# Attention scores of four pairs of heads in one issue, into four PSUM banks, instead of two pairs at a time into two

## The reference

```python
# 1: layer norm, attention with 16 heads of 16 over a sliding window of 128, output projection, MLP (GELU, 1024 wide)
scores = einsum('bhcqd,bhckd->bhcqk', qc, kcat) * scale     # own and previous chunk of 128 keys
out = einsum('bhcqk,bhckd->bhcqd', softmax(where(valid, scores, -inf)), vcat)
# 2: RWKV channel mix:  sigmoid(xr @ W_r.T) * (square(relu(xk @ W_k.T)) @ W_v.T)
# 3: Mamba: in-projection, convolution, then per channel (512) and state (16) over 256 channels of model width
hs = associative_scan((dA, BX)); y = einsum('blen,bln->ble', hs, Cm) + D * xc; out = (y * silu(z)) @ out_proj_w.T
# 4: one expert of 8 for each sequence, chosen by the mean of x: relu(x @ W1[top1] + b1) @ W2[top1] + b2
```

## Time and profile before

| | us |
|---|---|
| median of 3 runs (lowest, highest) | 3230.02 (3225.7, 3231.91) |
| time of the profiled execution | 3228.74 |
| its span, from the first to the last instruction | 3226.9 |
| PE busy / POOL / DVE / ACT | 2898.2 / 2642.7 / 2482.5 / 2391.9 |
| mean granted TensorE clock, as a share of full speed | 0.947 |

### The profile page before, as it was taken

How to read it: one execution, slowest core, us unless ns; L and a number is a source line. 1 busy time by engine, 2 the same in 40 slices (tenths; PEclk the granted TensorE clock), 3 DMA queues, 4 the chain that set the end, 5 groups by cost and what they waited for, 6 DMA issues and landing times.

```text
span 3226.9 us, 54604 instructions
## 1 busy us (share of the span) xinstructions
PE 2898.2 (90%) x17328; PEld 1833.4 (57%) x17328; DVE 2482.5 (77%) x5644; ACT 2391.9 (74%) x5299; POOL 2642.7 (82%) x1590
## 2 busy tenths in 40 slices
PE   5898888899999999999999999999999999988567
PEld 3565455475665656566565656656565655654246
DVE  3256978788787878879787887878787887879980
ACT  4587868787786878778687878878687787855432
POOL 1117999998998989999899989989998998988870
PEclk9999999899999999999999999999999999989788
DMA  3004453446445454644545364444545454455531
GB/s 82 14 35 144 145 164 111 158 146 206 131 143 173 153 182 140 205 145 147 184 127 198 127 210 141 169 153 149 190 128 197 149 179 140 151 182 180 176 124 41
DMA packets 285967, 477.31 MB, mean 148 GB/s; under 512 B 38451, under 2 KB 93363, under 8 KB 285683
## 3 DMA queue, kind: packets, MB, share of 16 engines
q1 hardware_dynamic: 285682, 473.83, 44.7%
HBM read 388.79 MB, written 84.93 MB: 147 GB/s over the span
## 4 chain that ended last, share of the span: by engine, by line
PE 70%; POOL 9%; ACT 8%; issue 6%; DVE 5%; DMA 2%; SPq 1%; ACTq 0%; DVEq 0%; POOLq 0%
PE bank L518 21%; PE bank L526 9%; PE bank L641 7%; PE bank L777 6%; PE bank L763 6%; PE bank L563 6%; PE bank L551 6%; PE bank L716 5%; POOL h_rows L1539 4%; POOL h_rows L1549 4%; PE bank L579 3%; ACT prob L832 2%; PE bank L512 2%; ACT zb L797 2%; DVE h_rows L1315 1%
## 5 line engine op out<-in xcount | busy, mean ns | idle before, releaser
L1539 POOL TENSOR_TENSOR h_rows<-u_rows,b_rows 128x1024 f32<-128x1024 f32 x512 | 1203.3, 2365 | 35.1 <-DMA b_rows<-bc_dram 34.4
L1549 POOL TENSOR_TENSOR h_rows<-h_rows,c_rows 128x1024 f32<-128x1024 f32 x480 | 1129.6, 2365 | 63.7 <-DVE state L1322 49.1
L1003 ACT ACTIVATE bank<-d_rows,a_rep 128x512 f32<-128x512 f32 x1024 | 682.5, 688 | 154.4 <-DMA d_rows<-delta_dram 44.3
L1315 DVE TENSOR_TENSOR_SCAN h_rows<-bank,state,h_rows 128x512 f32<-128x512 f32 x480 | 594.5, 1267 | 44.9 <-ACT bank L1003 30.1
L1315 DVE TENSOR_TENSOR_SCAN h_rows<-bank,h_rows 128x512 f32<-128x512 f32 x480 | 575.0, 1213 | 51.2 <-ACT bank L1003 40.0
L832 ACT ACTIVATE prob<-prob,neg_max 128x256 f32<-128x256 f32 x1024 | 509.4, 504 | 85.9 <-DVE neg_max L1098 85.8
L1098 DVE CUSTOM_DVE_ANT_0 prob<-bank,bands 128x256 f32<-128x256 f32 x896 | 335.9, 417 | 166.3 <-PE bank L551 162.4
L563 PE MATMUL bank<-ident,prob 128*128 128x128 f32 x2048 | 316.1, 281 | 61.3 <-ACT prob L832 55.1
L563 PEld LDWEIGHTS bank<-ident,prob 128*128 128x128 f32 x2048 | 235.8, 142 | 218.9 <-issue 199.7
L716 PE MATMUL bank<-h_rows,sum_n 128*32 128x512 f32 x2048 | 281.6, 625 | 70.7 <-POOL h_rows L1549 58.2
L518 PE MATMUL bank<-nb,w 128*128 128x512 f32 x512 | 270.7, 685 | 15.8 <-ACT nb L790 12.0
(11 more groups left out here) (164 smaller groups left out, 4847.8 us busy)
## 6 DMA issues: line engine op xcount, KB each, us to landing
u_rows<-u_dram SPq DMA_DIRECT2D x256, 256.0 KB, 3.9
d_rows<-delta_dram SPq DMA_DIRECT2D x256, 256.0 KB, 4.1
b_rows<-bc_dram SPq DMA_DIRECT2D x256, 256.0 KB, 3.1
c_rows<-bc_dram SPq DMA_DIRECT2D x256, 256.0 KB, 3.1
w<-in_W SPq DMA_DIRECT2D x28, 1024.0 KB, 7.1
zs_dram<-region_b SPq DMA_DIRECT2D x64, 256.0 KB, 2.8
xc_dram<-region_b SPq DMA_DIRECT2D x64, 256.0 KB, 3.5
u_dram<-region_b SPq DMA_DIRECT2D x64, 256.0 KB, 2.1
```

Of the source, the lines that this page charges most:

```text
L1003: e.activation(banks[at.bank][:, :], d_rows[:, c, :], ACT.Exp, scale=a_rep[:, k:k + 1]).then_inc(filled[at.bank], 1)
L1315: e.tensor_tensor_scan(rows, banks[at.bank][:, :], rows, start, ALU.mult, ALU.add).then_inc(drained[at.bank], 1)
L1539: e.tensor_tensor(half_of(i, b, half), u_rows[:, 2 * half:2 * half + 2, :], twice(b_rows[:, b % 2, :]), ALU.mult).then_inc(bx_ready.sem, 1)
L1549: e.tensor_tensor(rows, rows, twice(c_rows[:, b % 2, :]), ALU.mult).then_inc(hc_ready.sem, 1)
```

## The change

Four pairs are issued together at every eighth beat: the first head of each of the four, then the second head of each. So four row groups follow each other in PE's list, and four banks must be free before the first. The step in which DVE masks each pair stays where it was, so the two later pairs of such a quad hold their banks four beats longer. The functions that decide which scan quads VectorE finishes are rewritten as well (`vector_quads` for `vector_out`), with the same quads as before: none but the odd ones of the last two groups.

```diff
@@ uses_of, attention
         for n in range(32):
             v, odd = divmod(n, 2)
             at = ATT0 + 4 * v
-            out += [(f"s{n}", at, at + 1 + odd), (f"p{n}", at + 5 + odd, at + 6 + 2 * odd)]
+            out += [(f"s{n}", ATT0 + 8 * (n // 4), at + 1 + odd), (f"p{n}", at + 5 + odd, at + 6 + 2 * odd)]
@@ pe_attention
-            def scores_of(v):
-
-                if v == 0:
+            def scores_of(w):
+
+                if w == 0:
                     for name in ("q0", "q1", "k0", "k1"):
                         e.wait_ge(*gone(use(name)))
-                for n in (2 * v, 2 * v + 1):
+                for n in range(QUAD * w, QUAD * w + QUAD):
                     e.wait_ge(*free(use(f"s{n}")))
                 for par in range(2):
-                    for n in (2 * v, 2 * v + 1):
+                    for n in range(QUAD * w, QUAD * w + QUAD):
...
             for beat in range(AFTER - ATT0):
-                if beat % 4 == 0 and beat < 64:
-                    scores_of(beat // 4)
+                if beat % 8 == 0 and beat < 64:
+                    scores_of(beat // 8)
@@ the scan's choice of quads, in words the same as before
-def vector_out(i, b, batches):
-
-    return i >= 2 * batches - 2 and b % 2 == 1
+MIDDLE_QUADS, LAST_QUADS = (), tuple(range(1, QUADS, 2))
+def vector_quads(i, batches):
+
+    return LAST_QUADS if i >= 2 * batches - 2 else MIDDLE_QUADS
```

More of the change, by code:

```diff
@@ L110, with uses_of @@
 )
-def vector_out(i, b, batches):
-    return i >= 2 * batches - 2 and b % 2 == 1
-def uses_of(stage, shared=False):
+MIDDLE_QUADS, LAST_QUADS = (), tuple(range(1, QUADS, 2))
+def vector_quads(i, batches):
+    return LAST_QUADS if i >= 2 * batches - 2 else MIDDLE_QUADS
+def uses_of(stage, quads=()):
     if stage == "attention":
@@ L140, in uses_of @@
     if stage == "scan":
-        return ([(f"d{k}", SCAN0 + 2 * k + DECAY_AT, SCAN0 + 2 * k + (1 if shared and k // 4 % 2 else 0))
+        return ([(f"d{k}", SCAN0 + 2 * k + DECAY_AT, SCAN0 + 2 * k + (1 if k // 4 in quads else 0))
                  for k in range(TILES)]
@@ L179, in schedule @@
     for stage in PLACES:
[L180 to L183, removed]
+        for quads in ({(), MIDDLE_QUADS, LAST_QUADS} if stage == "scan" else {()}):
+            for name, first, last in uses_of(stage, quads):
+                begins.setdefault((stage, quads, first), []).append(name)
+                ends.setdefault((stage, quads, last), []).append(name)
     def earlier(thread, i):
@@ L196, in schedule @@
             _, _, stage, i, step = chain[0]
-            shared = stage == "scan" and vector_out(i, 1, batches)
-            names = begins.get((stage, shared, step), ())
+            quads = vector_quads(i, batches) if stage == "scan" else ()
+            names = begins.get((stage, quads, step), ())
             if len(names) <= len(idle) and not any(c in chains for c in earlier(*key)):
@@ L208, in schedule @@
             signalled[bank] += not (stage == "scan" and name[0] == "y")
-        for name in ends.get((stage, shared, step), ()):
+        for name in ends.get((stage, quads, step), ()):
             idle.append(uses[stage, i, name].bank)
@@ L455, in states_kept, with by_vector @@
             return state_ready.sem, CREDIT + (i // 2) * 2 * QUADS + (2 * QUADS if i % 2 else 2 * b + half + 1)
-        def out_formed(i, b):
[L459 to L463, removed]
+        quads_by = {"vector": [], "gpsimd": []}
+        for i in range(2 * BATCH):
+            for b in range(QUADS):
+                quads_by["vector" if b in vector_quads(i, BATCH) else "gpsimd"].append((i, b))
+        def by_vector(i, b):
+            return b in vector_quads(i, BATCH)
+        def out_formed(i, b):
+            if by_vector(i, b):
+                return hc_by_vector.sem, CREDIT + quads_by["vector"].index((i, b)) + 1
+            return hc_ready.sem, CREDIT + 2 * quads_by["gpsimd"].index((i, b)) + 2
         def fetched_again(i):
@@ L1310, in run_h @@
                 start = state[:, k:k + 1] if i % 2 else 0.0
-                if vector_out(i, k // 4, BATCH):
+                if by_vector(i, k // 4):
                     e.tensor_tensor_scan(banks[at.bank][:, :], banks[at.bank][:, :], rows, start,
@@ L1319, in keep_states @@
                 k = 4 * b + 2 * half
-                if not vector_out(i, b, BATCH):
+                if not by_vector(i, b):
                     e.wait_ge(*gone(use(f"d{k + 1}")))
@@ L1324, in times_c @@
             def times_c(k):
-                at, b, n = use(f"d{k}"), k // 4, k // 8 * 4 + k % 4
-                e.wait_ge(*h_in_bank.at(i - 2 * BATCH + 2, n + 1))
+                at, b = use(f"d{k}"), k // 4
+                e.wait_ge(h_in_bank.sem, CREDIT + 4 * quads_by["vector"].index((i, b)) + k % 4 + 1)
                 if k % 4 == 0:
@@ L1353, in dve_scan @@
                 k = tile_at(step, 1)
-                if k is not None and vector_out(i, k // 4, BATCH):
+                if k is not None and by_vector(i, k // 4):
                     times_c(k)
@@ L1553, in pool_scan @@
                     b = quad_at(step, OUT_AT + 2 * half)
-                    if b is not None and not vector_out(i, b, BATCH):
+                    if b is not None and not by_vector(i, b):
                         times_c(b, half)
```

## The result

The changed kernel takes 3311.82 us (median of 4 runs, 3309.13 to 3312.92) against 3228.86 us for the kernel before on the same chip: a ratio of 1.0255 (95% interval 1.0238 to 1.0271), so 83 us slower. The forecast was 3188 us, the upper end of the range 3248.

The account below looks back on a forecast made before the run. PE was taken to bound the kernel, with scores holding 181.5 us of the chain. A ceiling of 82 us less 23 and 13 for banks and 5 for the first 473 us left 41: 3188 us, range 3135 to 3248.

Parts of the forecast that it names:

- Four row groups side by side: PE's score matmuls: 16 instructions on four row groups take 1.09 us, against 1.06 for a burst of 8.
- The ceiling of 82 us: Most that PE's scores can gain: 45.3% of the 181.5 us they hold on the chain.
- p15: PE step whose bank comes free only after DVE masks pair 16 and runs two scans; 1.8 us in 13 groups.
- d32: A decay on ACT that now waits for a scan, about 1.3 us later than before; costed at nothing.
- The steps that changed places cost nothing: Steps moved in the list were costed at nothing; two ReLUs done earlier release a bank earlier.
- Some five more places, 1 us for the five together: Third and last quads, p27, a w_v product, an in-projection, an expert product get late banks; 13 us for 13 groups.
- 23 + 13 us for the banks: PE's waits for banks over 13 groups: 23 us at p15, 13 us at some five more places.
- the first 473 us: Opening stretch where DVE and ACT set the beat; half of its 10.3 us gain taken off, 5 us in the sum.
- The slower one: Rival: late banks work through a loop of quad, mask, decay, scan, transposes; 32 us slower, 3261 us, chance 0.16.
- The rule of the Trainium skill: Tiling speeds up TensorE but not PSUM evacuation; by it no gain, 3229 us; judged not to apply yet.
- DVE's wait for scores: Sign: DVE's waiting for PE's scores falls to about half of 118.8 us.
- The new wait before L572: Sign: PE waits for DVE's scan (L1324) before this line, near 1.8 us and once for a group.

Follow-up runs that it names:

- e9: The kernel before, with each score matmul taking only the first 128 of its 256 keys; 3162.72 us, ratio 0.979.
- e17: The whole change, with back taking its two banks just ahead of the copies and the expert's first product just ahead of its ReLU; 3268.04 us.
- e2: The change's order of steps, but two bursts, each pair's bank held as in the kernel before, banks handed out anew; 3269.09 us.
- e16: Step list of quads 0, 1, 2, 5, 6 together, but quad 1 in two bursts, its banks held as before, banks handed out anew; 3256.81 us.
- e18: Quads 0, 1, 2, 5, 6 together, others as before, with back taking its two banks later, just ahead of the copies; 3232.55 us.
- e5: The kernel before with only quads 0, 2, 5, 6 issued together, the others in two bursts, banks held as before; 3233.40 us.
- e7: The kernel before with the scan's decays in five SBUF buffers instead of banks, W_r standing in for four other weights; 4089.3 us, ratio 1.2652.

## Why the prediction was wrong

**Four row groups side by side: right.** 1.08 us for 16 instructions, and the line's busy time is 151.2 us where some 150 were expected.

**The ceiling of 82 us: right.** The rate of e9 gives 77. The share of a line in the chain was a good price for removing its time in the one case where no bank was touched.

**p15: right in place and size.** 1.64 us for 1.8, by the named loop, in e17 too. The three parts given for PE's way to p15 sum to 2.50 us, not 2.43, which makes it 1.74. d32, costed at nothing, cost nothing that shows: PE's wait behind the exponentials fell from 33.2 to 23.1 us.

**"The steps that changed places cost nothing": the step that failed first.** I had looked at what those steps release, and not at who stands behind them. A step moved forward on an in-order engine carries its own wait with it. Here ACT waited 2.63 us for PE with two decays behind, and scan and p4 behind these. e2 prices all moved steps at 36 us, e16 quad 1's at 26, each with its new hand-out of banks, and e18 gets quad 1's whole 43 back by moving one. By the shown rows p4 alone stands 2.88 us.

**"Some five more places, 1 us for the five together": the second.** In group 9 the last quad stands 1.31 us, p27 0.43, the in-projection 0.56 and the expert product 1.11; "the third" quad stands 0.56 us if it is quad 2, and 1.03 if it is quad 3; the product with w_v does not wait. That is 4.0 to 4.4 us in place of 1. The product with w_k, which I had not named, stands 2.53 us besides. Both bounds of that term had been given (9 us for a group above), and I took the lower one because "a wait at one place gives DVE time for the next". e5 shows the opposite: PE's gain at one quad is what brings it to the next place before that place's bank is free. How much of the 83 us these places cost is not parted from the moved steps by any run; e17 leaves 35 us with quads 3, 4 and 7.

**The sum.** In place of 23 + 13 us for the banks stand 135.7 us of waits in the middle, 11.7 us for a group, 0.2 before. The wait after the layer norm grew from 4.9 to 6.3 us for a group (58.9 us over 12, 72.7 over 11.6). Against the 7.2 us saved that leaves 5.7 us; the period grew by 6.5, and the 0.8 us between them stay open. The period that went with the forecast, 182.7 us, spreads the whole gain over 13 groups; the middle's own terms (5.5 us of scores less 2.8 for banks) give 183.1. Also the first 473 us gave 0.7 us, not 5: group 3's first scores stand at 472.3 instead of 473.0 us.

**The rivals.** The slower one names the loop (mask, decay on ACT, scan, transposes) and, with 8.8 us for a group, came nearest, but by p15-like places and without the moved steps. The rule of the Trainium skill (page TensorEngine Tiling (Array Packing), section Performance Considerations) holds evacuation to be what tiling can't speed up. The trace disagrees in this form: DVE, which reads out, is busy 152 us for a group as before, and its share of the middle fell from 82% to 79% (1822.92 and 1765.56 us). What came late was the single bank, not the work of reading out. What bears here is the same page's section Restrictions and Gotchas, by which row tiling raises the pressure on PSUM, since different row tiles write to different banks; the 135.7 us agree.

**The signs.** DVE's wait for scores fell to 76.3 us, more than half of 118.8. POOL's share fell to 88% where 93 was expected. The new wait before L572 came 35 times in the middle, about three times for a group (p4, p15 and p27 in the rows shown) and not once. The granted clock was 0.96 in the middle before and after, to the two digits shown, so it is no large part of the 6.5 us; in the first 473 us it was 0.92 for 0.94.

**Open.** Which of the waits left in e17 belongs to which of quads 3, 4 and 7, whether moved steps or later banks cause them, why the wait after the layer norm grew, and whether a list written for four-bank quads would keep some of the 77 us.

## What to carry to other kernels

A step that asks for more buffers at once is paid in two coins: waits on the buffers, and other steps that a planner moves to make room. List the moved steps, and for each ask what it waits for and what is queued behind it on its engine; one such step, with the shortage that moved it, was worth 44 us here, and one number of the table gave it back. Time taken off the leading engine returned in part (0.67) where no buffer was touched, and not at all in e5, where the next waits took it: check the next place that takes a buffer after each saving. When a change has equal parts, run subsets of them; here the losses of the quads nearly add up (43 + 27 + 18 for 83 us), and pointed to the step.

## What the runs showed of the hardware

With the decays in SBUF (e7), so that DVE's scan reads both operands from there, DVE and GpSimd both slow down (columns: busy us, mean ns of one, idle before):

```profile
L1544 POOL TENSOR_TENSOR h_rows<-u_rows,b_rows 128x1024 f32<-128x1024 f32 x512 | 1499.3, 2942 | 13.7 <-DMA b_rows<-bc_dram 13.7
...
L1320 DVE TENSOR_TENSOR_SCAN h_rows<-decay,state,h_rows 128x512 f32<-128x512 f32 x480 | 1114.0, 2352 | 22.6 <-issue 18.7 <-POOL h_rows L1544 2.3 <-DVE h_rows L1338 1.5
```

On average the scan takes 2352 ns, in the kernel before with its decay in a bank 1267; GpSimd's multiply takes 2942 ns, 2365 before. The shortest, the median and the longest scan (ns), in e7 and before:

```profile
L1320 DVE TENSOR_TENSOR_SCAN h_rows<-decay,state,h_rows x480: 1226/2516/3432, 495.6 to 3979.5; 128x512 f32<-128x512 f32 x160
...
L1315 DVE TENSOR_TENSOR_SCAN h_rows<-bank,state,h_rows x480: 1228/1273/1284, 439.9 to 3120.7; 128x512 f32<-128x512 f32 x160
```

The shortest are alike, and in 800 to 1200 us of e7 the scans beside which GpSimd did nothing took 1.22 and 1.28 us, so reading from SBUF is not slower in itself. The Trainium skill, page SBUF — State Buffer, section SBUF: two separate sides, says that a DVE instruction with two SBUF inputs and a GpSimd instruction that reads SBUF exclude each other. The trace agrees as far as both get longer, by 1085 and 577 ns on average; that one stands until the other has ended is not shown.
